# Message stage of a graph network kernel: ScalarE in place of the sync engine issues the loads of sorted edge attributes

## The chip, the cores and the metric

The kernel runs on one core of a Trainium2 chip. The metric is the device time of one execution in microseconds (us). The kernel before has a median of 1467.24 us over three runs.

The engines are named as in the profile: PE is TensorE (matmuls; PEld is its weight loads), DVE is VectorE, ACT is ScalarE, POOL is GpSimd, and SP is the sync engine, which does no arithmetic here and issues transfers. Every engine works through a program of its own, in order; they meet only at counting semaphores.

## The reference, cut to what matters

Four graph layers follow one another on 1250 nodes of 512 features, with 40,000 edges sorted by their destination. The third layer is the one whose message stage is changed. Cut to its core:

```
h  = softplus(edge_attr_20 @ W1 + b1) - log 2     # per edge, 20 -> 32
Wf = ((h @ W2 + b2) * edge_weight).reshape(E, 32, 6)
s, v = hs[dst], hv[dst]                            # rows of a node table, gathered per edge
edge = [s*y0*Wf0, (v.y)*Wf1, s*y*Wf2, v*y0*Wf3, ...]   # products with the edge's 4 numbers y
agg  = segment_sum(edge, src, n)                   # sums per source node
```

The fourth layer (two products with adjacency matrices and a tanh) comes behind it and needs the weights that SP loads near the end of the message stage.

## The kernel before, in words

Early in the kernel POOL scatters all edges, 32 words each, into a DRAM tensor `slots`, sorted by source node. The message stage then goes over them in 81 steps (`STEPS`). A step holds 4 chunks of 128 edges; four steps are a group, of which there are 21 (`RADIALS`), numbered `r`; step `st` has the place `s8 = st % 8` in a loop body of eight steps. A group's attributes come in one transfer of 256 KB, a "quad" of the tensor `at`, which has two halves: quad `q` lies in half `q % 2` until quad `q + 2` replaces it.

What each engine does in the stage:

- SP issues quads 0 and 1 at once. For quad `qn >= 2` it waits until POOL has read the indices of group `qn - 2` (`at_free`), PE has transposed them (`t_pe`) and DVE has decoded them (`y_ok`). Behind the last quad SP issues the small weights of the stage's end (L506 to L510) and the weights of the fourth layer, `wa` and `wb` of 1 MB each and two biases (L515 to L517).
- POOL (`gather_dst`, L929) issues three indirect gathers per step, 128 rows of the node table each, into a ring of 8 steps (`u`, for the first 8 steps `u_first`). Before the first gather of a group it needs that group's quad. At the second step of group r + 1 it waits for the gathers of group r and then counts up `at_free`.
- PE (`message`) makes at each step the edge weights of the next step (L1194, L1196) and adds up the messages of this one (L1220). Between these two, at the first step of group r, it transposes the quad of group r + 1 (L1205), for which that quad must have landed. L1211, L1179 and L1186 prepare group r + 1 in the steps that follow.
- ACT (`radial`) writes `py` for the next step (L731, four activations), and one further piece of group r + 1 at each step: L737, L741 to L746, L715 and L717, L722.
- DVE (`messages`, L1899 to L1915) makes the messages of a step from the gathered rows `u`, and at the end of a group's first step decodes the quad of the next group (L1930 to L1936). L1923 comes ahead of the messages of a group's last step.

The waits by which the edited code and its readers meet:

```python
pe.wait_ge(ld_at[rpar], loaded(r + 1, rpar))      # PE, first step of group r, ahead of L1205
dve.wait_ge(ld_at[rpar], loaded(r + 1, rpar))     # DVE, end of the same step, ahead of L1930
pool.wait_ge(ld_at[s8 // QUAD], there)            # POOL, ahead of the gathers of a step
after(pool, m_ok, used)                           # POOL at most 8 steps ahead of DVE
dve.wait_ge(u_in[s8], lap_u(st, s8, ...))         # DVE, ahead of L1899
```

Of the kernel before, what the change touches and what calls it, by code (L numbers as in the profile page):

```python
# [19 lines left out]
P = 128  # L20
# [18 lines left out]
QUAD = 4  # L39
# [3 lines left out]
STEPS = 81  # L43
PLACES = STEPS * QUAD
RADIALS = -(-STEPS // QUAD)
# [46 lines left out]
def graph_layers(nc, src, dst, dst_next, etype, norm, attr, x, bases, w_comp, h_bias, g_w1, g_b1, g_w2, g_b2,  # L92
# [14 lines left out]
    with ctx:  # L107
# [305 lines left out]
        def loaded(r, rpar):  # L413

            return (r - rpar) * 8 + 16
# [14 lines left out]
        def after(eng, s, value):  # L430

            if not isinstance(value, int) or value > 0:
                eng.wait_ge(s, value)

        block = ctx.enter_context(nc.Block())

        @block.sync
        def _(sp):

            sp.dma_start(dst_i[:, :], dst).then_inc(ld_tab, 16)  # L440
            sp.dma_start(src_i[:, :], src).then_inc(ld_tab, 16)
            sp.dma_start(next_i, dst_next).then_inc(ld_next, 16)
            for i in range(HALF):
                for n in (2 * i, 2 * i + 1):
                    sp.dma_start(x_in[0:rows(n), n, :], x[n * P:n * P + rows(n), :]).then_inc(ld_x[i], 16)
                if i == 0:
                    sp.dma_start(et_i[:, :], etype).then_inc(ld_et, 16)
            sp.dma_start(norm_f[:, :], norm).then_inc(ld_norm, 16)
            sp.wait_ge(const, 1)
            for q in range(QUAD):  # L450
                sp.dma_start(wc_blk[RELS * q:RELS * (q + 1), BASES * q:BASES * (q + 1)], w_comp).then_inc(ld_wc, 16)
            for n in range(BLOCKS):
                sp.wait_ge(ln_h, n + 1)
                sp.dma_start(h_rows[n * P:n * P + rows(n), :], x_in[0:rows(n), n, :]).then_inc(st_h, 16)

            sp.wait_ge(zero_ok, 1)
            for i in range(FILLS):
                if i < BLOCKS:
                    sp.wait_ge(rank_pe, i + 1)
                else:  # L460
                    sp.wait_ge(tile_pe, 4 * (i - BLOCKS + 1))
                sp.dma_start(slots[i * SLOTS // FILLS:(i + 1) * SLOTS // FILLS, :].rearrange(
                                 "(p a r) c -> p a (r c)", p=P, r=ZROW // ROW),
                             zero_t.unsqueeze(1).broadcast_to([P, SLOTS * ROW // P // FILLS // ZROW, ZROW]))\
                    .then_inc(st_zero, 16)

            sp.wait_ge(st_zero, 16 * FILLS)

            sp.wait_ge(half_pe, 1)

            def attributes(g, slot, lap):
                after(sp, st_att[slot], 16 * QUAD * lap)
                sp.dma_start(att_of[slot], attr[:, bass.ds(g * QUAD, QUAD), :]).then_inc(ld_att[slot], 16)

            def attribute_lap(i):
                for slot in range(ATTS):
                    attributes(ATTS * i + slot, slot, i)

            steps(sp, REAL_QUADS // ATTS, 1, 0, attribute_lap)
            for g in range(REAL_QUADS // ATTS * ATTS, REAL_QUADS):  # L480
                attributes(g, g % ATTS, g // ATTS)

            sp.wait_ge(adj_ok, BLOCKS)
            for slot in range(ATTS):
                sp.wait_ge(st_att[slot], ATT_DONE[slot])

            def sorted_quad(qn, par):
                if not isinstance(qn, int) or qn >= 2:
                    sp.wait_ge(at_free, qn - 1)
                    sp.wait_ge(t_pe, qn - 1)  # L490
                    sp.wait_ge(y_ok, qn - 1)
                sp.dma_start(at[:, par, :, :, :].rearrange("p s c w -> p (s c w)"),
                             slots[bass.ds(qn * QUAD * QUAD * P, QUAD * QUAD * P), :].rearrange(
                                 "(p t) w -> p (t w)", p=P)).then_inc(ld_at[par], 16)

            for qn in range(2):
                sorted_quad(qn, qn)

            def sorted_pair(i):
                for par in range(2):  # L500
                    sorted_quad(2 * i + par, par)

            steps(sp, RADIALS // 2, 1, 0, sorted_pair, skip=1)
            sorted_quad(RADIALS - 1, 0)
            sp.wait_ge(u_ev, BLOCKS)
            sp.dma_start(os_t[0:2 * HID, :], m_os).then_inc(ld_mq, 16)  # L506
            for i in range(2):
                sp.dma_start(ov_t[2 * HID * i:2 * HID * (i + 1), :], m_ov).then_inc(ld_mq, 16)
            sp.dma_start(qs_t, m_qs).then_inc(ld_mq, 16)
            sp.dma_start(qv_t, m_qv).then_inc(ld_mq, 16)  # L510

            sp.wait_ge(out_ok, AGG[2])
            sp.wait_ge(m_ok, RING)
            for t, w in ((wa, s_w1l), (wb, s_w1r)):
                sp.dma_start(t[:, :, :], w.rearrange("(k p) f -> p k f", p=P)).then_inc(ld_w3, 16)  # L515
            sp.dma_start(b_a[:, 0:KIN], s_b1).then_inc(ld_w3, 16)
            sp.dma_start(b_b[:, :], s_b2.to_broadcast([P, FEAT])).then_inc(ld_w3, 16)  # L517

            sp.wait_ge(lin_pe, 3 * BLOCKS)
            sp.dma_start(wa[:, :, :], s_w2l.rearrange("(k p) f -> p k f", p=P)).then_inc(ld_w3, 16)  # L520
            sp.wait_ge(pr_pe, TURNED)
            sp.dma_start(wb[:, :, :], s_w2r.rearrange("(k p) f -> p k f", p=P)).then_inc(ld_mq, 16)
            for n in range(BLOCKS):
                sp.wait_ge(out_ok, AGG[3] + n + 1)
                sp.dma_start(out[n * P:n * P + rows(n), :], low[0:rows(n), n % 2, :]).then_inc(st_o[n % 2], 16)
            for par in range(2):
                sp.wait_ge(st_o[par], 16 * BLOCKS // 2)

        @block.scalar
        def _(act):  # L530
# [180 lines left out]
            def radial(st, r, par, s8):  # L711

                if more(r + 1) and s8 % QUAD == 2:
                    act.wait_ge(near_pe, 2 * (r + 1) + 1)
                    nc.scalar.activation(at_t[:, :], ps[2][:, :], ACT.Abs, bias=row_neg[:, :]).then_inc(act_o, 1)  # L715
                    act.wait_ge(act_o, 3 * (r + 1) + 3)
                    nc.scalar.activation(hot_u[:, :], at_t[:, :], ACT.Relu, bias=1.0, scale=-1.0).then_inc(near_ev, 1)  # L717
                if more(r + 1) and s8 % QUAD == 3:
                    half = (s8 // QUAD + 1) % 2 * QUAD
                    act.wait_ge(near_pe, 2 * (r + 1) + 2)  # L720
                    after(act, m_ok, st - 3)
                    nc.scalar.activation(u_ring(st + 1)[:, half:half + QUAD, 0, :], ps[2].rearrange("p (s f) -> p s f", f=P), ACT.Copy)\  # L722
                        .then_inc(near_ev, 1)
                if valid(st + 1):
                    rn, rpar = (r + (s8 + 1) // QUAD - s8 // QUAD, (s8 + 1) // QUAD % 2)
                    act.wait_ge(w_pe, st + 2)
                    act.wait_ge(y_ok, rn + 1)
                    after(act, m_ok, st)
                    for c in range(QUAD):
                        q = (s8 + 1) % QUAD * QUAD + c  # L730
                        last = nc.scalar.activation(py[:, 1 - par, c, :], ps[1 - par][:, c * P:c * P + 2 * HID],  # L731
                                                    ACT.Copy, scale=yr[:, rpar, q, 0:1])
                    last.then_inc(p_ok, 1)
                if more(r + 1) and s8 % QUAD == 0:
                    act.wait_ge(t_pe, r + 2)
                    after(act, h_pe, r + 1)
                    nc.scalar.activation(at_t[:, :], ps[2][:, :], ACT.Copy).then_inc(t_act, 1)  # L737
                if more(r + 1) and s8 % QUAD == 1:
                    act.wait_ge(h_pe, r + 2)
                    after(act, h_ok, r + 1)  # L740
                    nc.scalar.activation(soft[:, 1, :], ps[2][:, :], ACT.Relu, bias=b1_c[:, :])  # L741
                    nc.scalar.activation(soft[:, 0, :], ps[2][:, :], ACT.Abs, bias=b1_c[:, :]).then_inc(act_o, 1)
                    act.wait_ge(act_o, 3 * (r + 1) + 1)
                    nc.scalar.activation(soft[:, 0, :], soft[:, 0, :], ACT.Exp, scale=-1.0).then_inc(act_o, 1)
                    act.wait_ge(act_o, 3 * (r + 1) + 2)
                    nc.scalar.activation(soft[:, 0, :], soft[:, 0, :], ACT.Ln, bias=1.0).then_inc(h_act, 1)  # L746

            scale_b = P ** -0.5
            for n in range(BLOCKS + 2):
# [21 lines left out]
            radial(*at_step(-3))  # L771
            radial(*at_step(-2))
            radial(*at_step(-1))
            message_steps(act, radial)

            act.wait_ge(m_pe, STEPS + 1)
            for i in range(0, HALF, 2):
# [1357 lines left out]
```

## Time and profile before

| | |
|---|---|
| median of 3 runs | 1467.24 us (1462.48 to 1468.37) |
| profiled execution | 1460.51 us, span 1458.7 us |
| PE busy | 1375.7 us (94%) |
| DVE busy | 865.4 us (59%) |
| ACT busy | 497.0 us (34%) |
| POOL busy | 890.9 us (61%) |
| mean granted TensorE clock | 0.979 of full speed |

The busy shares are means over stages with different limits. The message stage is only about a fifth of the span, from some 885 us to 1189 us, and has to be read by itself, with each engine's rows in order of time.

### The profile page before, as it was taken

How to read it: one execution, taken by the hardware profiler on the slowest of the kernel's cores; microseconds unless marked ns; L12 is line 12 of the kernel's file. 1: busy time of each engine (PE TensorE's matmuls, PEld its weight loads, DVE VectorE, ACT ScalarE, POOL GpSimd, SP SyncE). 2: the span in 40 equal slices, each digit the busy share in tenths (PEclk: the TensorE clock that was granted, in tenths of full speed). 3: DMA queues.
4: the chain of work that ended last, by engine and by line, in shares of the span. 5: the costliest groups of instructions: out<-in, count | busy, mean ns of one | idle time of the engine just before them, and what ended most of it. 6: DMA issues, size and time to landing. Idle time of an engine off the chain costs nothing. (4 is left out here: it accounts for less than half of the span.)

```text
span 1458.7 us, 24667 instructions
## 1 busy us (share of the span) xinstructions
PE 1375.7 (94%) x6924; PEld 938.6 (64%) x6925; DVE 865.4 (59%) x2485; ACT 497.0 (34%) x1279; POOL 890.9 (61%) x927
## 2 busy tenths in 40 slices
PE   4888899999999999999999998999999979999998
PEld 2788888888885433344595775666665656686565
DVE  8777745555555667766343337998888854411111
ACT  7000000000005887773621235565555546311100
POOL 5777777777777777777777767777777720000000
PEclk9999899999999999999999998999999989999999
DMA  4678789878885552223121122222222230000000
GB/s 164 192 229 232 222 290 321 255 240 258 268 263 160 162 169 76 77 77 117 33 57 25 35 61 62 69 62 66 73 66 66 83 80 1 29 1 29 8 29 36
DMA packets 104170, 173.00 MB, mean 119 GB/s; under 512 B 20155, under 2 KB 54128, under 8 KB 104080
## 3 DMA queue, kind: packets, MB, share of 16 engines
q0 software_dynamic: 42832, 103.15, 24.1%
q10 hardware_dynamic: 27790, 39.30, 8.8%
q1 hardware_dynamic: 33458, 29.39, 6.5%
q8 instruction: 51, 0.84, 0.2%
q14 instruction: 39, 0.32, 0.1%
HBM read 153.74 MB, written 18.02 MB: 118 GB/s over the span
## 5 line engine op out<-in xcount | busy, mean ns | idle before, releaser
L873 POOL DMA_INDIRECT gath<-h_rows,idx x313 | 303.1, 968 | 96.0 <-issue 65.8
L1007 PEld LDWEIGHTS ps<-spread,gath 128*128 128x128 f32 x2504 | 313.4, 201 | 68.5 <-issue 42.4
L1007 PE MATMUL ps<-spread,gath 128*128 128x96 f32 x2504 | 315.5, 285 | 23.6 <-DMA gath<-h_rows,idx 16.2
L1029 PE MATMUL ps<-base_t,z 128*128 128x512 f32 (+1 forms) x640 | 321.8, 614 | 0.0
L929 POOL DMA_INDIRECT u<-u_rows,at x219 | 218.9, 999 | 66.7 <-issue 62.5
L1546 DVE TENSOR_TENSOR z<-z,ps 128x384 f32 x313 | 172.4, 551 | 103.7 <-PE ps L1007 91.7
L899 POOL DMA_INDIRECT slots<-att,idx_s x160 | 161.1, 1007 | 49.5 <-issue 47.6
L899 POOL DMA_INDIRECT slots<-z,idx_s x153 | 154.4, 1009 | 43.9 <-issue 40.9
L1220 PE MATMUL ps<-msg,hot 128*128 128x256 f32 x648 | 160.6, 391 | 16.2 <-DVE msg L1915 14.7
L1220 PEld LDWEIGHTS ps<-msg,hot 128*128 128x128 f32 x648 | 118.5, 191 | 75.3 <-DVE msg L1915 54.1
L612 ACT ACTIVATE z<-ps 128x512 f32<-128x512 f32 x5 | 3.0, 597 | 411.0 <-PE ps L1029 410.9
L1723 DVE TENSOR_TENSOR cnt<-cnt,ps 128x120 f32 x313 | 88.2, 282 | 63.8 <-PE ps L1324 51.1
L620 ACT ACTIVATE hot_s<-iota_a,src_i 128x128 f16<-128x128 f16 x314 | 107.7, 390 | 37.4 <-PE ps L1324 33.6
L1029 PEld LDWEIGHTS ps<-base_t,z 128*128 128x128 f32 (+1 forms) x640 | 97.3, 188 | 33.7 <-issue 32.3
L731 ACT ACTIVATE py<-ps,yr 128x64 f32<-128x64 f32 x324 | 75.0, 314 | 99.9 <-PE ps L1196 89.8
L1089 PE MATMUL ps<-wa,ht 128*128 128x512 f32 (+1 forms) x240 | 104.8, 592 | 0.0
L1324 PEld LDWEIGHTS ps<-hot_d,hot_s 128*128 128x128 f16 x313 | 30.3, 97 | 107.8 <-issue 57.8
L1114 PE MATMUL ps<-adj,hs 128*128 128x384 f32 (+3 forms) x240 | 88.5, 369 | 0.0
L1114 PE MATMUL ps<-adj,hl 128*128 128x384 f32 (+3 forms) x240 | 84.6, 352 | 0.0
L1713 DVE TENSOR_SCALAR hot_d<-iota_a,acol 128x120 f16<-128x120 f16 x313 | 84.4, 271 | 0.0
L1101 PE MATMUL ps<-hs,adj 128*128 128x512 f32 (+1 forms) x200 | 83.9, 420 | 0.0
L1196 PE MATMUL ps<-w_blk,hid 128*128 128x512 f32 x162 | 83.7, 598 | 0.0
(297 smaller groups left out, 1902.1 us busy)
## 6 DMA issues: line engine op xcount, KB each, us to landing
base_t<-in_bases_dram ACTq DMA_DIRECT2D x116, 256.0 KB, 3.2
slots<-att SPq DMA_DIRECT2D x21, 256.0 KB
at<-slots SPq DMA_DIRECT2D x21, 256.0 KB, 2.7
gath<-h_rows,idx POOLq DMA_INDIRECT x313, 4.2
u<-u_rows,at POOLq DMA_INDIRECT x219, 2.5
att<-in_attr_dram SPq DMA_DIRECT2D x40, 64.0 KB, 2.0
slots<-att,idx_s POOLq DMA_INDIRECT x160
z<-in_attr_dram SPq DMA_DIRECT2D x39, 64.0 KB
```

The source lines that it names most:

```text
L620: last = nc.scalar.activation(hot_s[:, p % PAIRS, c, :], iota_a[:, 0:P], ACT.Abs, bias=src_neg[:, 2 * p + c:2 * p + c + 1])
L873: nc.gpsimd.indirect_dma_start(out=gath[:, c % RING, :], out_offset=None, in_=h_rows, in_offset=bass.IndirectOffsetOnAxis(ap=idx[:, par, c ...
L899: nc.gpsimd.indirect_dma_start(out=slots, out_offset=bass.IndirectOffsetOnAxis(ap=idx_s[0:r, turn_of, c:c + 1], axis=0), in_=att_of[slot][ ...
L929: nc.gpsimd.indirect_dma_start(out=u_ring(st)[:, s8, c + 1 - skip, :], out_offset=None, in_=u_soon if soon else u_rows, in_offset=bass.Ind ...
L1007: last = mm(bank[:, k * SPREAD:(k + 1) * SPREAD], gath[:, h_slot, k * P:(k + 1) * P], s_of.rearrange("p b d -> p (b d)"), start=True, stop ...
L1029: return mm(ps[BANKS[n]][0:rows(n), :], z[:, k, b, n * P:n * P + rows(n)], base_t[:, k, :], start=(t == JOINS[n]), stop=(t == JOINS[n] + T ...
L1089: last = mm(ps[6 + p % 2][0:r, :], ht[:, k, n * P:n * P + r], w[k], start=(k == 0), stop=(k == KIN - 1))
L1114: last = mm(bank[:, 0:b - a], part[0:rows(s), s, k * P:(k + 1) * P], graph[0:rows(s), s, a:b], start=(j == 0 and part is upper), stop=(j = ...
L1220: last = mm(acc[:, bass.ds(place[c], MSG)], hot[:, par, c, :], msg[:, par, c, :], start=False, stop=False)
L1546: v.tensor_tensor(zw, zw, bank[:, 0:KIN * SPREAD].rearrange("p (k b d) -> p k b d", k=KIN, b=BASES), ALU.add)\
L1713: v.tensor_scalar(hot_d[:, slot, 0:AWIN], iota_a[:, 0:AWIN], acol[:, bass.ds(t, 1)], None, ALU.is_equal)\
L1723: v.tensor_tensor(cw, cw, ps[5 + q % 2 * 2][:, 0:AWIN].rearrange("p (d s) -> p s d", s=BLOCKS), ALU.add)\
```

## The change

SP's waits and loads for quads 2 to 20 are taken out. ACT issues them: at the end of each group's last step (`s8 % 4 == 3`), behind all that `radial` does there, it waits for the same three semaphores with the same counts and then issues the load of the group two ahead. SP keeps quads 0 and 1; behind them it now waits until the last quad has landed before it goes on to the small weights. ACT's loop over the steps is shorter by one lap, so that the steps 72 to 80 are written out, where the counts are constants and no load past the last group is issued.

```diff
+        def sorted_quad(queue, qn, rpar):
+
+            queue.dma_start(at[:, rpar, :, :, :].rearrange("p s c w -> p (s c w)"),
+                            slots[bass.ds(qn * QUAD * QUAD * P, QUAD * QUAD * P), :].rearrange(
+                                "(p t) w -> p (t w)", p=P)).then_inc(ld_at[rpar], 16)
...
-            def sorted_quad(qn, par):
-                if not isinstance(qn, int) or qn >= 2:
-                    sp.wait_ge(at_free, qn - 1)
-                    sp.wait_ge(t_pe, qn - 1)
-                    sp.wait_ge(y_ok, qn - 1)
-                sp.dma_start(at[:, par, :, :, :].rearrange("p s c w -> p (s c w)"),
...
             for qn in range(2):
-                sorted_quad(qn, qn)
-
-            def sorted_pair(i):
-                for par in range(2):
-                    sorted_quad(2 * i + par, par)
-
-            steps(sp, RADIALS // 2, 1, 0, sorted_pair, skip=1)
-            sorted_quad(RADIALS - 1, 0)
+                sorted_quad(sp, qn, qn)
+
+            sp.wait_ge(ld_at[0], loaded(RADIALS - 1, 0))
             sp.wait_ge(u_ev, BLOCKS)
...
+                if valid(st) and more(r + 2) and s8 % QUAD == 3:
+                    act.wait_ge(at_free, r + 1)
+                    act.wait_ge(t_pe, r + 1)
+                    act.wait_ge(y_ok, r + 1)
+                    sorted_quad(nc.scalar, r + 2, s8 // QUAD)
...
-            message_steps(act, radial)
+            for st in range(8):
+                radial(*at_step(st))
+            with act.Fori(1, STEPS // 8 - 1) as i:
+                for s8 in range(8):
+                    radial(i * 8 + s8, i * 2 + s8 // QUAD, s8 % 2, s8)
+            for st in range(STEPS // 8 * 8 - 8, STEPS):
+                radial(*at_step(st))
```

## Rows read from the trace of the kernel before

**Rows 1.** Busy time by stretch; behind the engines: TensorE clock, DMA share, GB/s.
```profile
920.00:960.00 40.00, 39.61 (x195) 27.85 (x194) 38.04 (x115) 24.77 (x72) 31.16 (x30) 1.00 0.21 62
...
1040.00:1080.00 40.00, 37.80 (x179) 24.98 (x177) 35.40 (x109) 19.94 (x60) 30.25 (x33) 1.00 0.24 71
...
1176.00:1180.00 4.00, 3.97 (x14) 3.11 (x15) 3.93 (x11) 0.26 (x1) 2.11 (x3) 0.58 0.70 43
```

**Rows 2.** Who waited for whom from 900 to 1180 us.
```profile
POOL u L929 <- issue: 61.2, 201, 0.3
...
DVE vy L1899 <- DMA u<-u_rows,at: 25.6, 41, 4.5
```

**Rows 3.** The same list for SP's own queue, 850 to 1190 us.
```profile
SPq L492 <- POOLq L926: 245.4, 19, 16.4
```

**Rows 4.** POOL's gathers in order of time: start, us, engine, line, what, idle before.
```profile
893.43 0.96 POOL L929 DMA_INDIRECT u<-u_rows,at  x1 [0.31 <-issue]
...
903.66 1.93 POOL L929 DMA_INDIRECT u<-u_rows,at  x1 [0.30 <-issue]
...
984.78 0.96 POOL L929 DMA_INDIRECT u<-u_rows,at  x1 [0.30 <-issue]
...
1159.72 0.95 POOL L929 DMA_INDIRECT u<-u_rows,at  x1 [0.30 <-issue]
```

**Rows 5.** Timeline, steps 3 to 8, and SP's issue of quad 2.
```profile
876.79 0.34 SPq L492 DMA_DIRECT2D at<-slots  x1
...
896.08 0.55 DVE L1899 TENSOR_TENSOR vy<-u_first,yr 128x384 f32<-128x384 f32 x1
...
899.34 0.93 ACT L731 ACTIVATE py<-ps,yr 128x64 f32<-128x64 f32 x4 [0.48 <-PE ps L1196]
...
902.31 0.60 PE L1205 MATMUL ps<-ident,at 128*128 128x128 f32 x4
...
902.75 0.55 DVE L1899 TENSOR_TENSOR vy<-u_first,yr 128x384 f32<-128x384 f32 x1
...
909.84 0.55 DVE L1899 TENSOR_TENSOR vy<-u_first,yr 128x384 f32<-128x384 f32 x1
...
913.34 0.56 DVE L1899 TENSOR_TENSOR vy<-u,yr 128x384 f32<-128x384 f32 x1 [0.22 <-DVE msg L1915]
```

**Rows 6.** Timeline, steps 39 and 40, in the middle of the stage.
```profile
1022.94 0.95 POOL L929 DMA_INDIRECT u<-u_rows,at  x1 [0.30 <-issue]
...
1024.23 0.56 DVE L1899 TENSOR_TENSOR vy<-u,yr 128x384 f32<-128x384 f32 x1
...
1027.39 0.93 ACT L731 ACTIVATE py<-ps,yr 128x64 f32<-128x64 f32 x4 [0.48 <-PE ps L1196]
...
1030.28 0.60 PE L1205 MATMUL ps<-ident,at 128*128 128x128 f32 x4
```

**Rows 7.** SP's loads by source line: durations in ns, and issue to landing.
```profile
L492 SPq DMA_DIRECT2D at<-slots x21: 327/333/415, 854.3 to 1161.0; - x21
...
DMA to landing us min/median/max: 2.6/2.7/4.1
```

**Rows 8.** ACT's 256 KB loads in the first layer: timeline, and issue to landing.
```profile
588.18 0.42 ACT L624 ACTIVATE hot_s<-hot_s 128x256 f16<-128x256 f16 x1
588.40 0.34 ACTq L605 DMA_DIRECT2D base_t<-in_bases_dram  x1
...
DMA to landing us min/median/max: 2.6/3.2/5.8
```

**Rows 9.** Timeline of the stage's end, steps 77 and 80.
```profile
1164.48 0.39 SPq L515 DMA_DIRECT2D wa<-in_s_w1l_dram  x1
...
1166.08 1.00 POOL L929 DMA_INDIRECT u<-u_rows,at  x1 [0.30 <-issue]
...
1172.88 0.56 DVE L1899 TENSOR_TENSOR vy<-u,yr 128x384 f32<-128x384 f32 x1 [4.54 <-DMA u<-u_rows,at]
...
1184.23 0.56 DVE L1899 TENSOR_TENSOR vy<-u,yr 128x384 f32<-128x384 f32 x1 [0.41 <-ACT u L722]
```

More of the change, by code:

```diff
@@ L485, in _ @@
                 sp.wait_ge(st_att[slot], ATT_DONE[slot])
-            def sorted_quad(qn, par):
-                if not isinstance(qn, int) or qn >= 2:
-                    sp.wait_ge(at_free, qn - 1)
-                    sp.wait_ge(t_pe, qn - 1)
-                    sp.wait_ge(y_ok, qn - 1)
-                sp.dma_start(at[:, par, :, :, :].rearrange("p s c w -> p (s c w)"),
-                             slots[bass.ds(qn * QUAD * QUAD * P, QUAD * QUAD * P), :].rearrange(
-                                 "(p t) w -> p (t w)", p=P)).then_inc(ld_at[par], 16)
-            for qn in range(2):
-                sorted_quad(qn, qn)
-            def sorted_pair(i):
-                for par in range(2):
-                    sorted_quad(2 * i + par, par)
-            steps(sp, RADIALS // 2, 1, 0, sorted_pair, skip=1)
-            sorted_quad(RADIALS - 1, 0)
+            for qn in range(2):
+                sorted_quad(sp, qn, qn)
+            sp.wait_ge(ld_at[0], loaded(RADIALS - 1, 0))
             sp.wait_ge(u_ev, BLOCKS)
```

## The prediction, made before the result was known

> **What bounds the kernel now.** The whole page does not help, since the change lives in the message stage; so I read that stage by stretches, then the list of waits, then the timeline step by step.
>
> The stretches show two regimes [rows 1]. From 920 to 960 us DVE is busy 38.04 of 40 us and PE 39.61: arithmetic is the limit. From 1040 to 1080 us both are less busy (35.40 and 37.80). The list of waits says what changed [rows 2]: POOL waits for nothing but its own issue, 0.3 us before each gather, while DVE waits 41 times for gathered rows. A gather costs 0.95 us and the 0.3 us ahead of it, three make a step, so POOL's pace is the limit there. Measured over steps 30 to 76, whose first gathers start at 984.78 and 1159.72 us [rows 4], it is 174.94 / 46 = 3.80 us per step, 15.2 per group of four.
>
> In the first regime POOL is ahead. Its gathers of step 8 start at 893.43 us, DVE takes up step 8 at 913.34 [rows 4, 5]. In the second, the last gather of step 39 lands just as DVE starts that step: 1024.23 us against 1022.94 for POOL's start of step 40 [rows 6]. So DVE starts a step 3.80 + 1.29 = 5.1 us behind POOL's first gather of it when there is no lead left. The lead of 19.9 - 5.1 = 14.8 us is eaten up until step 30, after which every us that POOL is late moves the end of the stage.
>
> How fast was POOL before step 30? From step 8, (984.78 - 893.43) / 22 = 4.15 us per step, 0.35 more than later, though it waits for no semaphore [rows 2]: single gathers last longer, as the 1.93 us of the one at 903.66 [rows 4], in the stretch where DVE is busy nearly all the time [rows 1]. So POOL lost 22 x 0.35 = 7.7 us in that regime. DVE's own pace there is 3.5 us per step: step 30 starts 5.1 us behind POOL's 984.78, at 989.9, and (989.9 - 913.34) / 22 = 3.48, or 13.9 per group (13.76 from step 3 at 896.08 to step 7 at 909.84) [rows 4, 5].
>
> SP's loads wait nearly always for POOL's `at_free` [rows 3], that is for the landing of the group's last gathers, and never make anybody wait.
>
> **The change part by part.** The edit moves the issue to the end of ACT's part of a group's last step. All three semaphores have been up for a while there, so ACT stands still for none of them: in the middle of the stage `at_free` comes with 1024.23 us, and ACT's last `py` activations run from 1027.39 to 1028.32 [rows 6]. What moves is the time of the load, and four things hang on it.
>
> *ACT's own time.* 19 issues of 0.33 us [rows 7], 0.34 on ACT itself [rows 8], are 6.5 us on an engine that is busy 19.94 of 40 us [rows 1]. It lies in ACT's waits for PE. Cost 0; if that cover were gone, 6.5 us.
>
> *PE's transposes and DVE's decoding.* ACT's issue can begin before its last activation ends: at 588.40, 0.22 us into one that began at 588.18 [rows 8]. The last of the four `py` activations begins about 0.7 us after the first, so the issue comes some 0.85 to 0.95 us after `py` starts: at 900.2 us for quad 2 (899.34) and at 1028.3 in the middle (1027.39) [rows 5, 6]. Landing takes 2.7 us in this stage [rows 7]; ACT's loads of the same size took 3.2 under much heavier traffic [rows 8]. I take 2.7, since the traffic is the stage's, and keep 2.6 and their longest, 5.8, as ends. Quad 2 is then there at 902.9, where PE transposes it at 902.31 now: 0.6 to 0.7 us late. In the middle it is there at 1031.0 against 1030.28, 0.7 late. In the middle this is covered: the next DVE step starts only when its gathers have landed, and its inputs from ACT come over an us early. Cost 0. In the first regime nothing covers it: DVE's decoding stands ahead of the next step, and the arithmetic group becomes 13.9 + 0.7 = 14.6 us. That is still under POOL's 15.2, so it only delays the moment when the lead is gone.
>
> *POOL's start of step 8.* It needs quad 2, issued at 876.79 before and at 900.2 now [rows 5]. POOL starts step 8 at 902.9 in place of 893.43: 9.5 us later, with no work to fill the gap. For each later group the load is in time: in the middle it lands 8.1 us after POOL's start of the group, and is needed 15.2 us after it. At step 12, with DVE's lag, the quad comes at about 917.4 and POOL's own pace gives 918.1 or later.
>
> *What this gives back.* POOL's lead shrinks from 14.8 us to 914.0 - 902.9 - 5.1 = 6.0. At 4.15 us per step against 14.6 / 4 = 3.65 it is gone after 12 steps, with 3.5 for DVE after 9; I take 10. So POOL works against a gapless DVE for 10 steps, not 22, and loses 3.5 us there, not 7.7. Sum at step 30: 9.5 - 7.7 + 3.5 = +5.3 us. Bounds: +1.8 if the lead ends with no slow gathers, +6.0 with 12 steps of them.
>
> The trace shows the slow gathers first; the Trainium skill has a rule for them ("SBUF — State Buffer", "Who interferes with whom"): VectorE and GpSimd share a port pair by an exclusive lock, and one blocks while the other holds it. By that rule fewer slow gathers are to be expected with fewer steps of gapless DVE, as I have it; without it the +6.0 bound is the better guess.
>
> *The end of the stage.* SP's big loads go out at 1164.48 us and collide with the gathers of step 77: its last, issued at 1166.08, holds DVE until 1172.88, a wait of 4.54 us [rows 9], and PE, idle meanwhile, runs at 0.58 of its clock from 1176 to 1180 [rows 1]. After the change SP's chain is later by 4.1 us (ACT's place) and by 2.4 (it waits 2.7 us for quad 20 to land, where it now goes on after an issue of 0.33): without the +5.3, `wa` goes out at about 1171 us, where POOL starts step 79 (1159.72 + 3 x 3.80 = 1171.1). The same collision then takes the gathers of step 79. The last of step 77 landed 6.8 us after its start; that of step 79 starts at 1171.1 + 2.5 = 1173.6 and lands at 1180.4; one DVE step of 3.2 us later step 80 starts, at 1183.6, against 1184.23 now [rows 9]. I take 0; ends are -3.9 (no collision: step 80 then starts 2.6 us behind its last gather of 1177.7) and +2 (6.8 us behind it is 1184.5, and the slow clock falls on the last sums). The weights themselves are first used in the layer behind the stage.
>
> **Sum.** +5.3 + 0 + 0 = +5.3 us, 1460.51 to 1465.8 in the profiled execution. The median of the runs is 6.7 us above that execution; on the median, 1472.
>
> A page of the Trainium skill speaks against any effect: "DMA: Bandwidth & Descriptors", "Issuing engines are not separate DMA queues": all transfers run on the same 16 DMA engines whoever issues them, and the issuer saves only issue time. By it alone the sum would be 0, on the median 1467; this case's trace has a place in ACT's order that is later by 23.4 us for quad 2, which the rule leaves out.
>
> **The rivals.**
> 1. *The load becomes the loop's limit* (slower than before by over 0.5%). The loop is: DVE's last step of a group, ACT's issue 4.1 us after its start, landing L, PE's transposes, and 7.5 us from there to the next last step (902.31 to 909.84). That is 11.7 + L per group; it decides from L = 3.5 us on, where it passes 15.2. For it speaks ACT's 3.2 and the maximum of 4.1; against it the 2.7 of this stage. At 4.1 it costs 0.6 x 18 = 11 us, with the +5.3 some +16: 1483. At 5.8 it would be 2.3 x 18 = 41, but no load of this stage took that. Chance 0.12.
> 2. *No change.* POOL makes up the gap nearly whole (+1.8), or every step of the stage has enough slack somewhere: 1467 to 1469. For it: the lead of 14.8 us is more than the 9.5 lost. Against it: the lead is used up by step 30 now. Chance 0.14.
> 3. *The end gets better.* The big loads come too late for all but the last gathers, DVE's 4.54 us wait goes and the clock stays up: +1.8 - 3.9, about 1465. Chance 0.08.
>
> **How the numbers follow.** My forecast has 0.66; its own range is 1469 to 1476. 0.5% is 7.3 us, about what a measurement of this kernel can tell from no change. Over 1474.6 lie rival 1 and some 0.14 of my own case, 0.26; under 1459.9 nearly nothing, 0.03; between them 0.71. The range leaves out half of rival 1 and a little below rival 3: 1464 to 1482.
>
> **What would show it.** POOL's first gather of step 8 near 903 us, issued behind a wait for the load; the slow gathers of 1.9 us gone from about step 20 on, and DVE waiting for gathered rows from there; PE's L1205 about 0.7 us later within its group; the pace in the middle 3.80 us as before; DVE's long wait moved from step 77 to 79. The prediction is wrong if POOL waits for a load in every group, if the group in the middle is longer than 15.2 us, or if POOL's step 8 starts near 893 us.

## The result, and the profile after

The changed kernel takes 1474.53 us (median of six runs, 1471.62 to 1480.9) against 1465.36 us for the kernel before (six runs, 1462.48 to 1468.37). The ratio is 1.007, with a 95% interval of 1.0055 to 1.0086: slower, by 9 to 10 us where the prediction had 5.3.

| | after |
|---|---|
| profiled execution | 1474.14 us, span 1472.2 us (13.5 more than before) |
| PE, DVE, ACT, POOL busy | 1380.4, 868.3, 497.2, 890.0 us |
| mean granted TensorE clock | 0.983 |

The busy times moved by less than 5 us in PE and less than 3 us elsewhere, so the time is in waits. The lines of the code have moved: before's L929, L1899, L1205 and L731 are L932, L1902, L1208 and L723 here.

The start of the stage in the timeline of the kernel after (start, us, engine, line, what, idle before), where [rows 4, 5] stand for the kernel before:

```profile
900.90 0.55 DVE L1902 TENSOR_TENSOR vy<-u_first,yr 128x384 f32<-128x384 f32 x1
...
904.16 0.31 ACT L723 ACTIVATE py<-ps,yr 128x64 f32<-128x64 f32 x1 [0.48 <-PE ps L1199]
904.25 0.35 ACTq L437 DMA_DIRECT2D at<-slots  x1
904.27 0.56 DVE L1902 TENSOR_TENSOR vy<-u_first,yr 128x384 f32<-128x384 f32 x1
...
907.14 0.60 PE L1208 MATMUL ps<-ident,at 128*128 128x128 f32 x4
...
907.56 2.87 POOL L932 DMA_INDIRECT u<-u_rows,at  x1 [12.61 <-issue]
...
918.23 0.34 ACTq L437 DMA_DIRECT2D at<-slots  x1
...
922.54 0.17 DVE L1933 CAST dst_b<-at 128x4 bf16<-128x4 int32 x1 [1.07 <-DMA at<-slots]
922.55 0.65 PE L1208 MATMUL ps<-ident,at 128*128 128x128 f32 x4 [1.27 <-DMA at<-slots]
...
996.56 0.94 POOL L932 DMA_INDIRECT u<-u_rows,at  x1 [0.30 <-issue]
...
1172.28 0.95 POOL L932 DMA_INDIRECT u<-u_rows,at  x1 [0.31 <-issue]
```

POOL has nothing to do for 12.61 us ahead of its first gather of step 8. The profile calls this "issue", its word for idle time to which it can put no releaser, but the rows above it tell what POOL stood for: quad 2 was issued at 904.25, and PE transposed it from 907.14. From there step 8 starts 14.1 us later than at 893.43 [rows 4]. Step 30 starts at 996.56 and step 76 at 1172.28, 11.8 and 12.6 us later than before.

Busy time by stretch of the kernel after (PE, PEld, DVE, ACT, POOL; then TensorE clock, DMA share, GB/s), then one stretch of the kernel before, and the same stretch of `g2`, a run described below whose code is the kernel before's up to the end of the stage:

```profile
890.00:895.00 5.00, 5.00 (x14) 3.32 (x13) 3.81 (x14) 1.45 (x5) 4.21 (x3) 0.50 0.13 39
...
920.00:960.00 40.00, 36.91 (x168) 24.52 (x167) 35.06 (x108) 21.72 (x62) 31.11 (x30) 1.00 0.24 67
1040.00:1080.00 40.00, 37.35 (x172) 24.74 (x171) 34.41 (x105) 20.87 (x61) 30.55 (x32) 1.00 0.25 71
```

```profile
890.00:895.00 5.00, 5.00 (x24) 3.49 (x23) 4.91 (x17) 3.02 (x9) 4.08 (x4) 1.00 0.11 33
```

```profile
890.00:895.00 5.00, 5.00 (x12) 3.08 (x12) 3.90 (x15) 1.45 (x5) 3.78 (x4) 0.50 0.14 39
```

From 920 to 960 us DVE is busy 35.06 of 40 us, not 38.04 [rows 1]: the stretch in which arithmetic had no gaps now has some. From 1040 to 1080 little has changed. And from 890 to 895 us TensorE had a granted clock of 0.50 in this execution (1.2 GHz) and 1.00 (2.4 GHz) in that of the kernel before; this is a second thing, taken apart below.

Who waited for whom from 900 to 1190 us in the kernel after, and then the same list for SP's queue from 850 to 1200:

```profile
POOL u L932 <- issue: 74.8, 205, 12.6
DVE vy L1902 <- DMA u<-u_rows,at: 28.5, 45, 3.3
...
PE ps L1208 <- DMA at<-slots: 2.0, 2, 1.3
```

```profile
SPq L498 <- DMA at<-slots: 303.6, 1, 303.6
```

The loads of the kernel after by source line, and their time from issue to landing:

```profile
L437 ACTq DMA_DIRECT2D at<-slots x19: 339/340/354, 904.2 to 1176.8; - x19
...
DMA to landing us min/median/max: 2.5/2.7/4.2
```

Of POOL's 74.8 us, 12.6 are the one wait; the other 204 are the 0.3 us between gathers. The list puts only two waits of PE down to a quad, but it hides smaller ones: in the kernel before the transposes begin 0.86 us behind the product in front of them (L1196), or sooner, in every group; with the change they begin 0.93 us or more behind it (L1199) in 13 of 19 groups. The quad arrives just in time or a little late. SP stands in one wait of 303.6 us until quad 20 has landed. The one landing of 4.2 us is quad 3's (918.23 to 922.5): the group that holds it lasted 16.1 us, three later ones 14.6 to 14.9.

The end of the stage in the timeline of the kernel after, where [rows 9] stand for the kernel before:

```profile
1182.89 0.39 SPq L507 DMA_DIRECT2D wa<-in_s_w1l_dram  x1
...
1187.60 0.56 DVE L1902 TENSOR_TENSOR vy<-u,yr 128x384 f32<-128x384 f32 x1 [3.27 <-DMA u<-u_rows,at]
...
1192.59 0.56 DVE L1902 TENSOR_TENSOR vy<-u,yr 128x384 f32<-128x384 f32 x1 [1.29 <-DMA u<-u_rows,at]
...
1197.46 0.56 DVE L1902 TENSOR_TENSOR vy<-u,yr 128x384 f32<-128x384 f32 x1 [1.77 <-DMA u<-u_rows,at]
```

The weights go out at 1182.89, and the steps 78, 79 and 80 wait 3.27 + 1.29 + 1.77 = 6.3 us for gathered rows, where step 77 waited 4.54 [rows 9]. The difference of the spans adds up, each term as after minus before, counted from POOL's first gather of the stage (859.41 and 859.22, 0.2): +13.9 at step 8, -2.3 up to step 30, +0.8 up to step 76, +0.7 up to DVE's step 80, +0.3 behind it: 13.4, and with the 0.2 of the first gather 13.6, for 13.5 between the spans.

### The profile page after: what moved, and what is told of

It reads as the page before. It is cut to its first block, busy times and chain, and to the rows that moved or that the text cites. A ratio compares the mean times of both kernels' runs of the same rounds, so it can differ in the third digit from the quotient of the medians.

```text
span 1472.2 us, 24614 instructions
## 1 busy us (share of the span) xinstructions
PE 1380.4 (94%) x6924; PEld 934.2 (63%) x6925; DVE 868.3 (59%) x2485; ACT 497.2 (34%) x1279; POOL 890.0 (60%) x927
## 4 chain that ended last, share of the span: by engine, by line
PE 72%; DMA 10%; issue 5%; DVE 5%; ACT 3%; POOL 3%; ACTq 0%; DVEq 0%; POOLq 0%
PE ps L1032 17%; PE ps L1010 16%; PE ps L1092 9%; PE ps L1104 6%; PE ps L1117 6%; DMA gath<-h_rows,idx 5%; PE ps L1223 3%; DMA at<-slots 3%; DMA u<-u_rows,at 3%; PE ps L1314 2%; PE ps L1302 2%; POOL u L932 2%; PE ps L1199 2%; PE ps L1327 1%; PE ps L1083 1%
## 5 line engine op out<-in xcount | busy, mean ns | idle before, releaser
L1010 PEld LDWEIGHTS ps<-spread,gath 128*128 128x128 f32 x2504 | 308.2, 197 | 75.3 <-issue 43.1
L932 POOL DMA_INDIRECT u<-u_rows,at x219 | 217.0, 991 | 79.1 <-issue 75.1
L723 ACT ACTIVATE py<-ps,yr 128x64 f32<-128x64 f32 x324 | 75.0, 314 | 113.0 <-PE ps L1199 106.6
L1199 PE MATMUL ps<-w_blk,hid 128*128 128x512 f32 x162 | 84.5, 604 | 0.0
```

The source lines that it names most:

```text
L932: nc.gpsimd.indirect_dma_start(out=u_ring(st)[:, s8, c + 1 - skip, :], out_offset=None, in_=u_soon if soon else u_rows, in_offset=bass.Ind ...
L1010: last = mm(bank[:, k * SPREAD:(k + 1) * SPREAD], gath[:, h_slot, k * P:(k + 1) * P], s_of.rearrange("p b d -> p (b d)"), start=True, stop ...
L1199: mm(ps[1 - par][:, :], hid[:, rpar, q * P:(q + 1) * P], w2_blk[:, :], start=False, stop=True)\
```

## The experiments

**Theory A** is the one of the prediction: the place of the issue in ACT's order costs POOL its lead, and the time is lost once, at the start of the stage. Against it stand that the load holds up every group, that the engine that issues matters and not the place, and that the loss is at the stage's end.

### Four kernels on a chip where everything takes 2060 us

In `e0_after_again` nothing is edited: it is the changed kernel. In `e1_sync_issues_quad_2` and `e2_sync_issues_quads_2_to_7` (`SP_QUADS` 3 and 8), SP issues the first quads by before's rule; `e2` also writes out ACT's steps 0 to 23, not 0 to 7, since the quads of these steps need the exception:

```diff
 # the kernel after
             for qn in range(2):
                 sorted_quad(sp, qn, qn)
+            for qn in range(2, SP_QUADS):
+                sp.wait_ge(at_free, qn - 1)
+                sp.wait_ge(t_pe, qn - 1)
+                sp.wait_ge(y_ok, qn - 1)
+                sorted_quad(sp, qn, qn % 2)
...
-                if valid(st) and more(r + 2) and s8 % QUAD == 3:
+                if valid(st) and more(r + 2) and s8 % QUAD == 3 and not (isinstance(r, int) and r + 2 < SP_QUADS):
```

In `e3_sync_issues_at_scalars_place` SP issues every quad, but not before ACT has finished the `py` of the same step:

```diff
 # the kernel before
                     sp.wait_ge(y_ok, qn - 1)
+                    sp.wait_ge(p_ok, qn * 4 - 3)
...
             sorted_quad(RADIALS - 1, 0)
+            sp.wait_ge(ld_at[0], loaded(RADIALS - 1, 0))
```

> The changed kernel once more, as the measure for the three beside it. All theories expect a ratio near 1.007 to the kernel before. What is open is the part of the profiled difference that stood ahead of the load: TensorE ran at half clock until about 895 us in the changed kernel's profile and until about 886 in the one of before. If that is chance, this profile may show a return at about 886 us and GpSimd's step 8 at about 903 us, not 907.6; if it belongs to the change, it shows 895 again.

> SyncE issues quad 2 as before, ScalarE the quads from 3 on. Theory A (the loss is GpSimd's lead: each load that comes only at the end of ScalarE's step holds GpSimd once at the start of the group it is needed for): step 8 starts near 893 us again, but step 12 waits for quad 3, which ScalarE issues near 914 us, so that the wait moves from step 8 to step 12 and nearly all of the loss stays: ratio 1.005 to 1.007. Theory B (only the first load's lateness costs): ratio 1.000 to 1.002. Theory C (every load costs something in ScalarE's or TensorE's order): 18 of 19 loads are still late, ratio 1.0065.

> SyncE issues quads 2 to 7, which are all those that GpSimd needs while it is ahead (it has no lead left at step 30, in group 7); ScalarE issues quads 8 to 20. Theory A: the loss at the start is gone and only the stage's end is left, ratio 1.000 to 1.001 and GpSimd's step 30 at about 985 us. Theory C (every load costs): 13 of 19 loads are still ScalarE's, ratio about 1.005, and a step in the middle takes over 3.80 us.

> The kernel before, but SyncE waits in addition for the count that ScalarE puts up at the end of its part of a group's last step, and at the end for the last quad to land: the place in time of the change, without ScalarE issuing anything. If the place in time is the cause: ratio 1.007, perhaps 0.001 more because the count comes 0.6 us after the moment at which ScalarE issued. If the issue on ScalarE itself costs (its 0.34 us each, its longer program): ratio 1.000 to 1.002.

Measured, against 2057.62 us for the kernel before on that chip (31 runs): 2063.49 us (1.0027, 0.9992 to 1.0061), 2064.27 (1.0031, 0.9998 to 1.0064), 2065.69 (1.0049, 1.002 to 1.0078) and 2071.65 (1.0096, 1.0061 to 1.013). On this chip every kernel, the one before too, took some 2060 us, and what sets the pace there is something else. POOL's waits over the whole execution of the changed kernel there:

```profile
POOL u L932 <- issue: 177.2, 206, 17.7
```

That is 177.2 us for the same 206 waits that take 75.1 us in the execution shown above, one of them 17.7 us. The order of the four is told apart only at its ends (`e3` is slowest), and nothing about the steps of the prediction follows. The questions of `e1`, `e2` and `e3` are answered by the same kernels on other chips: `i1`, `f2` and `g1` below.

### f2: SP issues quads 2 to 7, ACT the other thirteen

The edit is that of `e2` above.

> The kernel of e2 once more, since the chip of that call ran every kernel in some 2060 us, with engines waiting for their own issue. SyncE issues quads 2 to 7, ScalarE quads 8 to 20. Theory A (the loss is GpSimd's lead at the start): ratio 1.000 to 1.001, GpSimd's step 30 near 985 us. Theory C (every load issued by ScalarE costs): about 1.005, and a step in the middle takes over 3.80 us.

Measured: 1466.62 us (12 runs) against 1463.71 (17 runs), 1.0021 with an interval of 1.0009 to 1.0033; span 1467.5. The timeline of `f2`: POOL's step 8, and DVE's steps 79 and 80.

```profile
895.25 0.94 POOL L938 DMA_INDIRECT u<-u_rows,at  x1 [0.30 <-issue]
...
1188.22 0.56 DVE L1908 TENSOR_TENSOR vy<-u,yr 128x384 f32<-128x384 f32 x1 [3.88 <-DMA u<-u_rows,at]
1191.40 0.56 DVE L1908 TENSOR_TENSOR vy<-u,yr 128x384 f32<-128x384 f32 x1
```

POOL waits for no load: step 8 starts 34.38 us after the stage's first gather (34.21 before, 48.15 after), step 30 at 125.71 (125.56 before, 137.15 after). So 13 of ACT's 19 issues stand where the change puts them, and some 70% of the loss is gone (0.21% left of 0.70%, where 0 to 0.1% was expected).

One number seems to speak for the rival that every group pays: from step 30 to step 76 `f2` takes 3.90 us per step, and step 76 starts 305.14 us after the first gather, 4.6 us behind the kernel before (300.50). The trace of `g2`, in which ACT issues no load and TensorE's clock came back as late as in `f2`, answers it: there step 76 starts at 304.30. So all but 0.8 us of the 4.6 came with the late clock, and from step 44 to step 76, with the lead gone in both, a step takes 3.82 us in `f2` and 3.82 in `g2`. It is not ACT's time, and not something that each group pays. At the end DVE waits 3.88 us at step 79, and its step 80 starts 7.8 us behind the last gather, 6.48 before.

### g1: SP in ACT's place, for every quad

The edit is that of `e3` above.

> The kernel of e3 once more, on a chip that hopefully runs the kernel before in 1465 us: SyncE issues every load, but waits in addition for the count at the end of ScalarE's part of a group's last step, and at the end for the last quad to land. If the place in time is the cause: ratio 1.007 to 1.008, GpSimd's first gather of step 8 about 8 us or more behind where the kernel before has it relative to its step 0 (34.2 us). If ScalarE's issue itself costs: ratio 1.000 to 1.002.

Measured: 1480.89 us (6 runs) against 1462.2 (17 runs), 1.0129 with an interval of 1.0108 to 1.015; span 1477.5. The engine is the old one and the time is worse than with the change. The timeline of `g1`:

```profile
903.26 0.66 PE L1207 MATMUL ps<-ident,at 128*128 128x128 f32 x4 [0.66 <-DMA at<-slots]
...
903.95 1.00 POOL L931 DMA_INDIRECT u<-u_rows,at  x1 [10.68 <-issue]
...
918.51 0.65 PE L1207 MATMUL ps<-ident,at 128*128 128x128 f32 x4 [0.86 <-DMA at<-slots]
...
1011.52 0.65 PE L1207 MATMUL ps<-ident,at 128*128 128x128 f32 x4 [0.68 <-DMA at<-slots]
...
1027.10 0.65 PE L1207 MATMUL ps<-ident,at 128*128 128x128 f32 x4 [0.73 <-DMA at<-slots]
```

The list of waits of `g1`, 900 to 1190 us:

```profile
PE ps L1207 <- DMA at<-slots: 14.8, 19, 1.1
...
DVE dst_b L1932 <- DMA at<-slots: 10.6, 19, 0.8
```

SP's wait ends when the last `py` activation has ended, 0.93 us or more after the first began, where ACT's own issue goes out 0.09 us after it began. That later moment, about 1 us, is enough: PE now waits for the quad in all 19 groups, DVE waits for gathered rows nowhere before step 78, and a group lasts from one L1207 to the next, 1027.10 - 1011.52 = 15.6 us in the middle, 918.51 - 903.26 = 15.25 at the start, and 15.5 on average over the stage, against POOL's 15.2. The time is 1.29% over the kernel before, where 0.7 to 0.8% was expected. The landings have not changed (median 2.7 us). This is rival 1's loop, reached by a later issue and not by a slower load: from DVE's last step of a group to the issue 4.35 us, from there to the transposes 2.8, and from these to the next last step 8.3 to 8.4.

### h1: ACT issues one step earlier

```diff
 # the kernel after
-                if valid(st) and more(r + 2) and s8 % QUAD == 3:
+                if valid(st) and more(r + 2) and s8 % QUAD == 2:
```

> The changed kernel, but ScalarE issues each load at the end of a group's third step, not of its last. Theory A (the place in time is all, the lead of GpSimd is lost at the start): the load of quad 2 comes some 3.4 us earlier (a DVE step), GpSimd's step 8 begins 3.4 us earlier relative to its step 0 (about 45 us behind it where TensorE's clock comes back late, 41 where it comes back early), and PE and DVE no longer wait for a quad at the first step of a group; ratio 1.003 to 1.005. Rival (the issue on ScalarE costs, wherever it stands): ratio 1.007. Second rival (in the middle GpSimd's count is not up yet at that place, ScalarE stands and holds py back): the pace in the middle rises over 3.80 us per step, ratio over 1.007.

Measured: 1468.79 us (7 runs) against 1462.88 (18 runs), 1.004 with an interval of 1.0024 to 1.0055; span 1466.9. Its timeline:

```profile
898.85 0.34 ACTq L437 DMA_DIRECT2D at<-slots  x1
...
902.27 1.08 POOL L932 DMA_INDIRECT u<-u_rows,at  x1 [9.62 <-issue]
```

Neither PE nor DVE waits for a quad, but POOL's step 8 still waits 9.62 us. It starts 42.92 us after the first gather, 5.2 less than with the change, of which 2.2 are the clock's (step 3 of DVE at 39.26 for 41.49); at step 30 the difference to the kernel before is 131.76 - 125.56 = +6.2, and the time is between the two kernels. The loss follows the moment of the issue.

### i1: SP issues quad 2 alone

The edit is that of `e1` above.

> The kernel of e1 once more: SyncE issues quad 2 early as before, ScalarE the quads from 3 on. Theory A (a load at the end of ScalarE's step holds GpSimd at the first group for which its lead reaches that far): step 8 begins some 34 to 36 us behind step 0, and the wait moves to step 12, so that steps 12 and 30 stand where the changed kernel has them: 63 to 66 and 135 to 137 us behind step 0; ratio 1.005 to 1.007. Theory B (only the first load counts): ratio 1.001 to 1.003.

Measured: 1474.11 us (6 runs) against 1462.13 (17 runs), 1.008 with an interval of 1.0066 to 1.0094; span 1469.0. Handing back the one load that POOL had waited for gains nothing that the two medians show. POOL in the timeline of `i1`, the last gather of step 11 and the first two of step 12:

```profile
911.36 0.94 POOL L938 DMA_INDIRECT u<-u_rows,at  x1 [0.30 <-issue]
919.47 2.96 POOL L938 DMA_INDIRECT u<-u_rows,at  x1 [7.17 <-issue]
922.74 0.94 POOL L938 DMA_INDIRECT u<-u_rows,at  x1 [0.30 <-DVE msg L1924]
```

Step 8 is on time (34.98 after the first gather), and step 12 waits 7.17 us for quad 3, the first one that ACT issues. Step 12 starts 58.08 us after the first gather, and step 30 starts at 132.09. Both are sooner than was expected (63 to 66, and 135 to 137); the clock came back sooner here than with the change (DVE's step 3 at 37.63 for 41.49), which is 3.9 us of it. Beside `i2` (described below), whose start is the kernel before's and whose clock came back at the same moment (step 3 at 37.68), step 12 is 8.1 us late, step 30 7.2 and step 76 6.6.

The lead is not lost at a step, it is capped: a load that goes out at the end of group r lets POOL start group r + 2 no sooner than some 3.3 us after DVE has started group r + 1 (904.27 to 907.56 with the change), whichever quad is the first.

### g2, i2, h2: what the end costs

`g2_weights_after_step_79` holds the large weights back until DVE is through step 79:

```diff
 # the kernel before
             sp.wait_ge(out_ok, AGG[2])
-            sp.wait_ge(m_ok, RING)
+            sp.wait_ge(m_ok, STEPS - 1)
```

> The kernel before with one edit: SyncE holds the fourth layer's weights (1 MB twice and two biases) back until DVE has made the messages of step 79, by when the last gathers have landed. If the long wait near the end (4.54 us at step 77 before, 6.3 us over three steps after the change) is the collision with these loads: step 80 starts 2.6 us behind its last gather, not 6.5 or 7.4, TensorE stays at full clock, ratio 0.996 to 0.998. If it is something else: 1.000. If the weights then come too late for the fourth layer: above 1.000. Its start is the kernel before's, so its profile also shows when TensorE's clock comes back there (886 or 895 us).

Measured: 1464.12 us (12 runs) against 1462.2 (17 runs), 1.001 with an interval of 0.9998 to 1.0021, and not the 0.996 to 0.998 that a collision with the weights alone would have given. Step 77 no longer waits, but the steps 79 and 80 do. The stretches of `g2`:

```profile
1176.00:1178.00 2.00, 2.00 (x11) 1.63 (x11) 1.35 (x5) 1.97 (x5) 1.39 (x3) 1.00 0.13 35
...
1180.00:1182.00 2.00, 2.00 (x14) 1.70 (x15) 0.79 (x2) 0.91 (x5) 1.45 (x2) 1.00 0.77 53
1182.00:1184.00 2.00, 1.58 (x13) 0.72 (x9) 2.00 (x8) 0.98 (x3) 0.46 (x1) 1.00 0.88 33
```

and its timeline, POOL's last gather and what follows it:

```profile
1181.51 0.95 POOL L929 DMA_INDIRECT u<-u_rows,at  x1 [0.30 <-issue]
...
1184.77 0.39 SPq L515 DMA_DIRECT2D wa<-in_s_w1l_dram  x1
...
1187.04 0.56 DVE L1899 TENSOR_TENSOR vy<-u,yr 128x384 f32<-128x384 f32 x1 [2.35 <-DMA u<-u_rows,at]
```

No weight is in flight before 1184.77, and yet the DMA engines are 0.77 to 0.88 busy with 53 and 33 GB/s, where 0.13 went with 35 GB/s just before. These are the gathers of the last steps. There are 81 x 512 = 41,472 slots and 40,000 edges; a slot without an edge keeps the fill value, all of whose words are zero, so its index is 0, and 128 such slots fetch row 0 of the node table 128 times. `i2_spread_padding` makes the index word of the fill value the number of the partition; this changes which row an empty slot fetches, and nothing else, since its weight stays zero and so does what it adds:

```diff
 # the kernel before
-            sp.wait_ge(zero_ok, 1)
+            sp.wait_ge(zero_ok, 2)
...
             nc.scalar.activation(zero_t, epsb[:, :].to_broadcast([P, ZROW]), ACT.Copy, scale=0.0).then_inc(zero_ok, 1)
+            act.wait_ge(zero_ok, 1)
+            nc.scalar.activation(zero_t.bitcast(i32).rearrange("p (a w) -> p a w", w=ROW)[:, :, DSTC],
+                                 row_neg[:, :].to_broadcast([P, ZROW // ROW]), ACT.Copy, scale=-1.0).then_inc(zero_ok, 1)
```

> The kernel before with the padding's gathers spread over 128 rows alone; SyncE's big loads go out where they did. If the repeated row is what makes the last gathers slow and the big loads only add to it: step 77 still waits for its rows (4 us or so), step 80 then starts where arithmetic allows, ratio 0.998 to 0.999. If the two edits of h2 are each worth nothing alone: 1.000. If the repeated row is all: 0.9975 as h2.

Measured: 1462.67 us (11 runs) against 1462.13 (17 runs), 1.0 with an interval of 0.9989 to 1.0011: nothing gained by this edit alone. Step 77 still waits, by 4.18 us, since the weights collide with its gathers as before. `h2_spread_padding_late_weights` has both edits:

> The kernel before with two edits at the end of the stage. The unfilled slots, whose gathers all fetch row 0 of the node table (their edge weight is 0, so the row does not matter), get the partition's number as index, so that the 128 gathers of such a chunk fetch 128 rows; and SyncE holds the big weights back until step 79 is done, as in g2. In g2 the gathers of steps 79 and 80 landed 3.9 and 5.5 us behind their issue though no other transfer ran. Theory: rows fetched 128 times from one place are slow, so that step 79 and 80 now land after 2.6 to 2.8 us and TensorE keeps its full clock: ratio 0.994 to 0.997. Rival: something else is slow there: as g2, 1.001.

Measured: 1459.37 us (12 runs) against 1462.88 (18 runs), 0.9977 with an interval of 0.9965 to 0.9989, a little less than the expected 0.994 to 0.997; span 1457.2. The same stretches in `h2`:

```profile
1176.00:1178.00 2.00, 1.63 (x9) 0.65 (x7) 2.00 (x9) 1.94 (x4) 1.70 (x2) 1.00 0.21 66
...
1180.00:1182.00 2.00, 2.00 (x17) 1.27 (x16) 1.67 (x6) 0.71 (x2) 0.75 (x1) 1.00 0.25 66
1182.00:1184.00 2.00, 1.72 (x8) 1.16 (x7) 1.54 (x4) 0.82 (x4) 0.00 (x0) 1.00 0.28 69
```

and its last gather and DVE's step 80:

```profile
1179.79 0.97 POOL L932 DMA_INDIRECT u<-u_rows,at  x1 [0.30 <-issue]
...
1182.46 0.56 DVE L1902 TENSOR_TENSOR vy<-u,yr 128x384 f32<-128x384 f32 x1 [0.79 <-DMA u<-u_rows,at]
```

Step 80 starts 2.67 us behind its last gather, where `g2` has 5.53 and the kernel before 6.48. The two edits gain only together; this version beats both kernels, the one before by 0.1 to 0.35%.

### i3: the change with the clean end

The changed kernel with the two edits of `h2`.

> The changed kernel with h2's two edits at the end of the stage. If the change costs at the start alone (GpSimd's lead) and the end adds what is its own there: it stands some 8 to 9 us over h2, ratio to the kernel before 1.003 to 1.004, steps 78 to 80 land 2.6 to 2.8 us behind their issue. If a part of the change's cost sits at the end (the later big loads), it comes closer to h2: 1.001 to 1.002.

Measured: 1466.49 us (5 runs) against 1462.13 (17 runs), 1.0034 with an interval of 1.0021 to 1.0047; span 1463.1. In the timeline of `i3` POOL still waits at step 8, and DVE starts step 80 only 2.53 us behind the last gather (1186.62):

```profile
904.31 2.98 POOL L935 DMA_INDIRECT u<-u_rows,at  x1 [12.53 <-issue]
...
1189.15 0.56 DVE L1905 TENSOR_TENSOR vy<-u,yr 128x384 f32<-128x384 f32 x1 [0.65 <-DMA u<-u_rows,at]
```

With both ends clean the change costs 1.0034 / 0.9977 = 1.0057, 8.3 us on the medians' scale (each against its own runs of the kernel before). The spans differ by 5.9, but 1.1 of the missing 2.4 us lie ahead of the stage and 0.8 behind it: from the stage's first gather to DVE's step 80 it is 330.35 us in `i3` and 322.57 in `h2`, 7.8 more. That is the price of the start by itself.

## Why the prediction was right in kind and short in size

**POOL starts step 8 late: right.** The wait is there, at the step and for the reason given; `f2` removes it and most of the loss, `i1` moves it by a group, `h1` shortens it, `g1` has it with the other engine. Predicted +9.5, measured +13.9 from the stage's first gather. By parts: the issue was 3.35 us behind DVE's step 3, not 4.1, since ACT lets it go 0.09 us into `py` and not 0.85 to 0.95 (-0.8); from issue to POOL's gather it took 3.3, not 2.7, of which 0.3 is POOL's own time ahead of a gather (+0.6); and DVE's step 3 was itself 4.6 us late.

**That 4.6 us is the clock's, and it is not the change's.** The granted clock stood at 0.50 from 890 to 895 us. `f2` shows the same 0.50 there, and `g2`, whose code is the kernel before's up to the end of the stage, reaches step 3 42.14 us after the first gather against 36.86 before and 41.49 after; in `g1` it is 37.75. So it varies from one execution to another. With the lead gone it shows at once, since POOL's start of step 8 follows ACT, and ACT follows PE. With the lead whole it hardly shows at step 30 (126.79 in `g2`, 125.71 in `f2`, 125.56 before), but it is not free there either: at step 76 `g2` is 3.8 us behind the kernel before (304.30 for 300.50). Each of these is one execution, but the kernel before was profiled in one whose clock came back early, and the kernel after in one where it came back late, and that widens the difference between the two profiles. Beside `g2`, with a clock as late (step 3 at 42.14 for 41.49), the change is 12.8 us late at step 8, 10.4 at step 30 and 8.6 at step 76 (312.87 for 304.30), not 13.9, 11.6 and 12.4; that is close to the 9.2 of the medians. Why the clock comes back at different times was not settled.

**The lead shrinks, and its loss ends at step 30: right in kind, over-credited in size.** The prediction gave back 7.7 - 3.5 = 4.2 us of slow gathers. From step 8 to step 30 POOL took 996.56 - 907.56 = 89.0 us, where 22 x 3.80 would be 83.6: it lost 5.4, and 2.3 were given back. The term counted 10 steps at 0.35 us; DVE's first wait for gathered rows came at step 22, after 14. And it left out that POOL can restart together with DVE: the first gather after the wait took 2.87 us, as in `i3` (2.98) and `i1` (2.96), each begun within 0.2 us of a DVE step and released at its end (the next gather's releaser is `DVE msg`). But this one gather is not the whole of the 1.9 us too much: in `h1`, where it began 0.3 us behind DVE's step, it took 1.08, and the 22 steps still took 88.8 us, with four later gathers of 1.9. What decides how many gathers are slow was not settled.

The Trainium skill's rule ("SBUF — State Buffer", "Who interferes with whom": VectorE and GpSimd share a port pair under an exclusive lock) fits these rows: single gathers of 1.9 to 3.0 us, ending with DVE's operation, and fewer of them where DVE has gaps. The fit is not whole: the same section says that `tensor_tensor`, which is all that DVE runs beside the 2.87 us gather, was not seen to stall transfers. No run here took DVE's work away, so the lock itself is argued, not shown.

**The arithmetic group grows to 14.6 us: right in size, by two errors that cancel.** Between steps 11 and 23 groups of 14.6 to 14.9 us were measured. The transposes were 0.1 to 0.2 us late there, not 0.7, since the issue came 3.5 us behind DVE's last step and not 4.1. But from the transposes to the next last step it took 8.3 to 8.5 us, not the 7.5 read from the kernel before: the late quad is handed on from PE to ACT, and DVE waits for ACT's `low` (L738) 0.65 us at 930.36 and 0.69 at 944.96, where it had waited 0.16 to 0.30. The sum is 3.5 + 2.9 + 8.3 = 14.7. So in these groups the loop of rival 1, through the load, already set DVE's pace, some 0.3 to 0.6 us under POOL's 15.2. Quad 3, at 4.2 us from issue to landing, made one group 16.1.

**The pace in the middle is unchanged: right.** (1172.28 - 996.56) / 46 = 3.82 us per step for 3.80.

**The end costs nothing: wrong in its working, though inside its bounds.** `wa` went out where it was forecast, at POOL's start of step 79 (1182.89 and 1183.72), but the collision did not move from one step to one other step. Three steps waited 6.3 us in all, for 4.54. The prediction had missed that the gathers of the last steps are slow by themselves, as `g2` and `h2` show. Taking the end clean from after to `i3` gains 1.007 - 1.0034, 0.36%, and from before to `h2` 0.23%: the end of the change is worse by about 0.13%, 2 us. That difference is within the intervals; the profiles have 1.0 us behind step 76 (0.7 + 0.3).

**The rivals.** Rival 1, the load as the loop's limit, did not decide the time in the middle of the stage, but it was near: `g1` reaches it with an issue 1 us later, and with the change itself the loop takes 14.6 to 14.9 us beside POOL's 15.2. The prediction let it decide from a landing of 3.5 us on; by the parts measured in `g1` it does so there from 2.5. That the change's issue is early enough is luck: ACT lets the load go at the first of its four `py` activations, which the prediction had not foreseen. Rival 2, no change, falls: 1.0055 is the lower end. Rival 3 falls too: the weights came late, and the gathers that they met were worse ones. The rule that the issuing engine saves only issue time (the Trainium skill, "DMA: Bandwidth & Descriptors", "Issuing engines are not separate DMA queues") is borne out as far as it goes: with the moment held 1 us later the old engine was no better (`g1`), and 13 loads issued by ACT cost nothing that shows in a step (`f2` beside `g2`); no run has the old engine at the very same moment. It is silent on the moment, and that was all of the effect.

The sum as measured in the medians, about +9 to +10: some +8 for the start (`i3` against `h2`) and +2 for the end, in place of +5.3 and 0. The term that was short is the start, and within it the price of POOL's late step 8 and what the shorter lead gives back. The forecast of 1472 us lies nearer to the measured 1474.5 than +5.3 does to +9.2, and that is luck: it started from a median of three runs, 1467.24, where six gave 1465.36.

## What to carry to other kernels

A load issued early is a buffer between two engines, and its worth is the lead that it allows the reader; an issue put behind another engine's work of the same iteration caps that lead for good, however many of the later loads arrive in time. So place it by the earliest moment at which its buffer is free, count how far ahead the reader was, and look for what the lead was hiding (here slow gathers and, in part, a late return of the clock). Where a transfer moves little and takes long, look at the addresses before looking for a competitor.

## What the runs showed of the hardware

- Indirect gathers whose rows are nearly all the same are slow by themselves: with empty slots on row 0, the last gather landed 5.5 us after its issue (an upper bound from DVE's start) with DMA engines 0.88 busy at 33 GB/s; with the rows spread over 128 it was 2.7 us, at a share of 0.25 to 0.28 and 66 to 69 GB/s.
- ScalarE's queue issued a transfer 0.09 us after an activation that stands ahead of it in the program had begun, at 904.25 and again at 918.23; at 588.40 [rows 8] it was 0.22 us into one. So its place in the timeline is that of the first of four short activations, not of the last.
- The granted clock's return to 1.00 at the start of the stage varied by over 5 us between executions of code that is the same up to there (from 890 to 895 us it was 1.00 in the kernel before and 0.50 in `g2`). With it VectorE's step 3 moved by up to 5.3 us (36.86 to 42.14 after the first gather), and POOL's step 76 by 3.8.
- One chip ran all of these kernels, the one before among them, in about 2060 us, with a mean granted clock of 0.839 for 0.983 and engines waiting on their own issue; differences of some 10 us are not seen there as they are elsewhere.
